# Second expert stage of a two-layer transformer kernel: second products four pairs behind, work grouped in PSUM banks

## The reference, cut to what matters

```python
logits = -dist2 + jnp.einsum('bld,ed->ble', x, rw) + rb
topv, topi = jax.lax.top_k(logits, TOP_K)            # TOP_K = 4 of E = 16
w = jax.nn.softmax(topv, axis=-1)
hidden = jax.nn.gelu(jnp.einsum('bld,efd->blef', x, w1) + b1, approximate=False)
exp_out = jnp.einsum('blef,edf->bled', hidden, w2) + b2
fused = jnp.sum(w[..., None] * take_along_axis(exp_out, topi[..., None], axis=2), axis=2)
```

## Time and profile before

| | us |
|---|---|
| three runs, median | 649.49 |
| lowest and highest of the three | 643.33, 649.77 |
| profiled execution, its own time (the span) | 724.3 |
| of it, from 461 us to 701 us: second expert stage | 240 |

### The profile page before, as it was taken

The page is one execution under the profiler, slowest core; times in us unless marked ns, Lnnn a source line. Parts: engine busy times, 40 slices in busy tenths (PEclk is TensorE's granted clock), DMA queues, the critical chain, the costliest instruction groups (busy, mean ns, idle before and its releaser), DMA issues.

```text
span 724.3 us, 15939 instructions
## 1 busy us (share of the span) xinstructions
PE 551.5 (76%) x4812; PEld 383.9 (53%) x4812; DVE 446.3 (62%) x1659; ACT 363.8 (50%) x972; POOL 323.3 (45%) x429
## 2 busy tenths in 40 slices
PE   5789999994129736899999992598877787759980
PEld 2234445443018734445554451387766686759880
DVE  5678889835752237678999658576544554423257
ACT  2158888841005634388998732144433343335543
POOL 3755765130025755624333424444555544554440
PEclk9999999975558975689999965589999889978995
DMA  6520620021001261750400010434433333334473
GB/s 179 150 65 11 185 58 1 2 44 19 1 12 43 39 142 63 213 167 10 124 2 2 2 44 18 138 123 131 133 120 116 110 122 115 126 101 155 163 234 112
DMA packets 65734, 65.11 MB, mean 90 GB/s; under 512 B 16259, under 2 KB 46099, under 8 KB 65526
## 3 DMA queue, kind: packets, MB, share of 16 engines
q1 hardware_dynamic: 58390, 52.49, 22.9%
q0 software_dynamic: 7264, 11.62, 6.6%
HBM read 29.77 MB, written 11.87 MB: 57 GB/s over the span
## 4 chain that ended last, share of the span: by engine, by line
PE 56%; DVE 14%; issue 7%; another core or an unknown queue 7%; ACT 7%; POOL 3%; SPq 3%; DMA 2%; DVEq 0%; ACTq 0%; POOLq 0%
PE bank L896 9%; PE bank L1311 8%; PE bank L1301 7%; PE bank L879 6%; PE bank L861 4%; ACT queries L1600 3%; PE bank L913 3%; DVE passed L1882 2%; ACT prob L1423 2%; PE bank L1097 2%; PE bank L937 1%; PE bank L1255 1%; PE bank L1109 1%; POOL sum L761 1%
## 5 line engine op out<-in xcount | busy, mean ns | idle before, releaser
L1700 DVE TENSOR_REDUCE mx<-bank 128x2 f32<-128x512 f32 x256 | 163.3, 685 | 37.7 <-PE bank L861 35.9
L1423 ACT ACTIVATE prob<-bank 128x512 f32<-128x512 f32 x256 | 142.1, 601 | 42.0 <-PE bank L879 37.3
L1600 ACT ACTIVATE queries<-bank,prob 128x128 f32<-128x128 f32 x316 | 90.1, 377 | 137.2 <-remote 65.5
L1301 PE MATMUL bank<-keys,prob 128*128 x632 | 98.1, 305 | 14.1 <-ACT keys L1592 12.0
L1301 PEld LDWEIGHTS bank<-keys,prob 128*128 128x128 f32 x632 | 88.2, 216 | 19.3 <-issue 18.4
L774 POOL DMA_INDIRECT prob<-xs,idx_g x64 | 61.7, 964 | 80.4 <-DVE idx_g L2113 23.5
L1311 PE MATMUL bank<-W,queries 128*128 x632 | 94.6, 296 | 3.4 <-issue 1.9
L1311 PEld LDWEIGHTS bank<-W,queries 128*128 128x128 f32 x632 | 83.6, 205 | 5.6 <-issue 3.3
L783 POOL DMA_INDIRECT parts<-augs,idx_s x64 | 63.2, 987 | 45.8 <-DVE augs L2154 23.3
L896 PE MATMUL bank<-prob,augs 128*32 128x256 f32 x1024 | 82.5, 409 | 1.4 <-ACT prob L1423 1.4
L861 PE MATMUL bank<-keys,queries 32*128 32x256 f16 x512 | 78.2, 294 | 4.2 <-DVE mx L1700 2.0
(11 more groups left out here) (272 smaller groups left out, 1017.3 us busy)
## 6 DMA issues: line engine op xcount, KB each, us to landing
prob<-W SPq DMA_DIRECT2D x79, 258.0 KB
W<-in_w SPq DMA_DIRECT2D x48, 256.0 KB, 3.7
sum<-zero SPq DMA_DIRECT2D x3, 1024.0 KB, 9.5
xr<-XT SPq DMA_DIRECT2D x12, 128.0 KB, 2.0
xs<-X SPq DMA_DIRECT2D x2, 768.0 KB, 5.7
prob<-xs,idx_g POOLq DMA_INDIRECT x80
XB<-sum SPq DMA_DIRECT2D x1, 1024.0 KB, 5.1
Y<-sum SPq DMA_DIRECT2D x4, 256.0 KB, 5.8
```

What stands on the lines that cost most here:

```text
L1301: last = nc.tensor.matmul(bank[2 + p % 2][:, P * f:P * f + P], wc[:, p % 4, P * f:P * f + P], xsT2[:, bass.ds(at, 1), :], start=True, stop ...
L1423: nc.scalar.activation(prob[:, v % 8, :, :], st_bank(b, v)[:, :], ACT.Exp, scale=SCALE).then_inc(exp_done, 1)
L1600: last = nc.scalar.activation(hid2[:, p % 4, f, :], bank[2 + p % 2][:, P * f:P * f + P], ACT.Gelu, bias=wc[:, p % 4, WB + f:WB + f + 1])
L1700: nc.vector.tensor_reduce(m_at, bank[S1B[u % 2]][:, :].rearrange("p (j k) -> p j k", j=2), AX.X, ALU.max).then_inc(s1_used, 1)
```

## The change

- The second product of pair p moves from step p + 2 to step p + 4 (SKEW). First products get four PSUM banks (2 to 5) instead of two, so first product p waits for gelu p - 4. The hidden activations get eight buffers instead of four (`queries` and `XT`), since gelu p now waits for second product p - 8.
- Turns are grouped: tiles 0 and 1 alone, then [2, 3], [4, 5], [6, 7], then fours. A group is transposed into one bank and copied by one ACT instruction. The group [8..11] is turned at step 6, and the next ones at 9, 11, 14, 17 and 20; from tile 32 on a group that starts with tile t is turned at step t - 3.
- Lists from tile 6 on go in groups of three in one bank: three lists every two steps to tile 32, then three every three steps. One copy and one conversion serve three.
- Outputs are grouped: four second products go to one bank, and DVE adds the four pairs at the step that is five after the group's last pair, once the last of the four is there. The last groups are [76, 77] and [78].
- Buffers move to make room (`gateT`, `hit`, the third slice of choices). SP's load of that slice waits for first product 62. The order on POOL and SP is as before, their waits too but for that one.

```diff
-def turn_step(t):
-    if t < RING:
-        return -1 if t == 0 else -((12 - 11 * t) // 16)
-    return min(t - 2, 21 - -(4 + 11 * (t - 31)) // 8)
-def list_step(t):
-    if t < 6:
-        return -1
-    return 2 * (t - 6) // 3 if t < RING else t - 14
+TURN_GROUPS = [[0], [1], [2, 3], [4, 5], [6, 7]] + [list(range(t, t + 4)) for t in range(8, NJT[1], 4)]
+FIRST_LISTS, PER_LIST = 6, 3
+LIST_GROUPS = [list(range(t, min(t + PER_LIST, NJT[1]))) for t in range(FIRST_LISTS, NJT[1], PER_LIST)]
+OUT_GROUPS = [list(range(p, p + 4)) for p in range(0, 76, 4)] + [[76, 77], [78]]
+SKEW, HRING, HIDRING = 4, 4, 8
+def turn_step(group):
+    t = group[0]
+    if t < 8:
+        return {0: -1, 1: 0, 2: 1, 4: 3, 6: 4}[t]
+    return -((1 - 11 * t) // 16) if t < RING else t - 3
+def list_step(g):
+    return 2 * g if g < 9 else 3 * g - 8
+SUMS = {p: [g for g, group in enumerate(OUT_GROUPS) if group[-1] + SKEW + 1 == p] for p in range(NPAIR + SKEW + 1)}
...
+            def row_turns(group):
+                wait_for(pe, rows_in, group[0])
+                for i, t in enumerate(group):
+                    row_fetched(pe, t)
+                    nc.tensor.transpose(bank[0][:, P * i:P * i + P], xg[:, t % XRING, 0:P],
+                                        ident[:, :]).then_inc(row_turned, 1)
...
             def pair_first(e, p):
-                if p >= 2:
-                    pe.wait_ge(pair_gelu, p - 1)
+                if p >= HRING:
+                    pe.wait_ge(pair_gelu, p - HRING + 1)
...
             def pair_second(e, p):
                 pe.wait_ge(pair_gelu, p + 1)
-                if p >= 2:
-                    pe.wait_ge(pair_added, p - 1)
+                g, i = OUT_OF[p]
+                if i == 0 and g >= 2:
+                    pe.wait_ge(pair_added, OUT_GROUPS[g - 2][-1] + 1)
...
-                for p in range(NPAIR + 2):
+                for p in range(NPAIR + SKEW):
...
-                    if p >= 2:
-                        pair_second(expert.pop(p - 2), p - 2)
+                    if p >= SKEW:
+                        pair_second(expert.pop(p - SKEW), p - SKEW)
...
-            def pair_sum(s, p):
+            def pair_sum(s, p, g):
-                dve.wait_ge(pair_out, p + 1)
+                dve.wait_ge(pair_out, OUT_GROUPS[g][-1] + 1)
...
-                    if p >= 2:
-                        e = pair_expert(dve, words, p - 2)
-                        s = pair_slot(dve, e, p - 2)
-                        pair_gated(e, s, p - 2)
-                        pair_sum(s, p - 2)
+                    for g in SUMS[p]:
+                        for n in OUT_GROUPS[g]:
+                            e = pair_expert(dve, words, n)
+                            s = pair_slot(dve, e, n)
+                            pair_gated(e, s, n)
+                            pair_sum(s, n, g)
```

More of the change, by code:

```diff
@@ L194, in program @@
         yo = rt[:, 4 * P:8 * P].rearrange("p (b c) -> p b c", c=P)
[L195 removed]
+        hid2 = [h[:, :].rearrange("p (s f c) -> p s f c", s=4, f=NF)[:, s, :, :] for h in (queries, XT) for s in range(4)]
         xsT2 = keys[:, :].rearrange("p (t c) -> p t c", c=P)
@@ L1316, in pair_steps @@
             def pair_steps():
-                for t in LISTS[-1]:
+                for t in range(FIRST_LISTS):
+                    if t >= 2:
+                        pe.wait_ge(row_ready, t - 1)
                     row_list_of(t)
@@ L1322, in pair_steps @@
                 words = pair_tables(pe, pe_words)
-                for t in TURNS[-1]:
-                    row_turn(t)
+                for group in TURNS[-1]:
+                    row_turns(group)
                 expert = {}
-                for p in range(NPAIR + 2):
+                for p in range(NPAIR + SKEW):
                     if p < NPAIR:
@@ L1606, in pair_steps @@
                 for p in range(NPAIR):
-                    for t in TURNS[p - 1]:
-                        row_in(t)
+                    for group in TURNS[p - 1]:
+                        rows_copied(group)
                     pair_hidden(p)
@@ new lines, in rows_listed @@
+            def rows_listed(g):
+                t0, n = LIST_GROUPS[g][0], len(LIST_GROUPS[g])
+                dve.wait_ge(row_list, t0 + n)
+                if g == 0:
+                    dve.wait_ge(row_ready, t0)
+                for t in LIST_GROUPS[g]:
+                    row_hits(t)
+                ends_of = bank[1][:, 0:(P + 2) * n].rearrange("p (t c) -> p t c", c=P + 2)[:, :, P + 1]
+                nc.vector.tensor_copy(slot_expert[:, t0:t0 + n], ends_of).then_inc(lstep, 1)
+                dve.wait_ge(lstep, NJT[0] + 2 * FIRST_LISTS + (PER_LIST + 1) * g + n + 1)
+                at = t0 % (2 * PER_LIST)
+                nc.vector.tensor_copy(idx_g[:, t0:t0 + n], tok[:, at:at + n, 0]).then_inc(row_ready, n)
```

112 lines of the change are left out of this document (65 added, 47 removed).

## The result

| | us |
|---|---|
| before, four runs beside those of the change: median, range | 646.41 (642.87 to 649.77) |
| the change, four runs: median, range | 669.87 (666.28 to 672.46) |
| ratio, with its 95% interval | 1.0344 (1.0277 to 1.041) |
| profiled execution of the change, its span | 667.3 |

The change is slower by 22 us by the ratio and 23.5 by the medians. A ratio leaves out runs more than 1.5% above the fastest of their kernel and a median doesn't, so the two can differ by 2 to 3 us. The forecast was 662, 12.3 us slower, in a range from 645 to 668: the direction was right, the size was about half.

The account below looks back on a forecast made before the run. PE and POOL were taken as level near full use, POOL's 1.29 us per indirect DMA deciding. Later sums and turn waits put the last scatter at 642.8 against 630.5, so 649.5 + 12.3 = 662 us, range 645 to 668.

Parts of the forecast that it names:

- The runs have none of the late releases: Second expert stage: waits where PE was done but others learned late (46 us of PE idle) are nearly absent from runs.
- The supposition on what lies ahead of this stage: First expert stage, ahead of the second: supposed disturbed by the same waits; no size given.
- The profiled span falls because four banks absorb the late releases: Four banks and the longer skew absorb these waits, so profiled span falls from 724.3 to some 690 to 715.
- Start and steps to 24: Second expert stage: step 3 starts 2 us earlier; step 18 at 504.6 against 506.6, step 24 at 516.3.
- Early turns starve PE, 2.8 us: Early turns in groups of four: waiting for gathers stalls PE 0 to 5 us in all, taken as 2.8.
- Sums in fours: "Nothing", but later: DVE lags 3 us at most, costing nothing; but sum 15 comes at step 20, sum 16 at step 24.
- Why scatter 1 is late: POOL: scatters 1 to 4 wait for sums 16 to 19; scatter 1 at 517.5, where before scatter 0 started at 507.9.
- POOL's 1.29 us per DMA up to gather 63: POOL issues DMAs back to back, 1.29 us each: 61 from scatter 1 put gather 63 at 596.2.
- Turns from tile 32 on: PE waits for gathers at turned groups: 1.6 us at [36..39], then 2.2 at each of the six that follow.
- The first rival: POOL keeps up: a DMA takes under 1.04 us, no turn waits, no change; 647 us (643 to 655), chance 0.24.
- the second (faster): Waits of the two-bank scheme are in the runs too, the change removes them: 640 us (625 to 643), chance 0.12.
- The third: Early turns starve PE as well, 5 us in place of 2.8, plus half clock: +16 to +20, 667 us, chance 0.12.

Follow-up runs that it names:

- the repeated profile: The kernel before, unchanged, profiled again: 647.66 us beside 648.13, ratio 0.9989, span 647.0.
- c3: The change itself, run again in a later session where every kernel was slower: 735.42 us beside 723.77 for before, ratio 1.0222.
- a1: The change with sums one by one, at the step of their second product: 660.02 us beside 646.59 for before, ratio 1.0236.
- a3: The change with sums one by one and turns from tile 32 on at step t - 1: 658.88 us, ratio 1.0251 to before.
- a4: The change with single sums, turns from tile 32 on at step t - 1 and a skew of two pairs: 657.22 us, ratio 1.0181 to before.
- a8: The change with three 128x128 fills on POOL ahead of each scatter: 719.88 us beside 649.1 for before, ratio 1.1123.
- b3: The kernel before with one 128x128 fill on POOL ahead of each scatter: 652.58 us beside 648.13, ratio 1.0101.
- a6: The change, single sums, skew two, groups from tile 32 turned at before's step for their last tile or earlier t - 1: 652.89 us, ratio 1.0079.
- a2: The change with turns from tile 32 on at step t - 1 in place of t - 3: 668.7 us, without a ratio.
- a7: The change with single sums, skew two, earlier turns of groups from tile 32 on, and 11 gathered tiles in flight: 652.47 us, ratio 1.0061 to before.
- a9: The change with single sums, skew two, turns in twos at before's step for the second tile: 722.9 us beside 719.56, ratio 1.0038.
- d1: The change with single sums, skew two, turns in twos and 11 gathered tiles: 720.75 us beside 714.33 for before, ratio 1.0097.

## Why the prediction was right in sign and half in size

**The runs have none of the late releases.** Right, and now seen: the repeated profile has no such wait. What was not seen is that an execution of this kind can be that of a whole session, runs and profile alike. Whether the first profile was taken in the session of its runs is not on record. The supposition on what lies ahead of this stage was right: 9.3 us of the 77.3 lie there.

**The profiled span falls because four banks absorb the late releases.** Wrong, though the span fell. The two executions were of different conditions. Like beside like, the span goes from 724.3 to 732.1 (c3) and from 647.0 to 667.3, and ACT's remote waits from 65.5 us to 85.9 (44.4 + 41.5). The stage loses 14.8 us there (240.3 to 255.1) and 17.9 in the quick condition.

**Start and steps to 24.** Right as differences. Step 3 was to start 2 us earlier: 10.8 against 12.6. Step 18 was put 2.0 us ahead of before: 1.7. The levels were too low, by 2.6 and 2.9 us at step 18 (45.7 against 48.3, 43.7 against 46.6), since I took 2.2 us a step from 3 to 18, and before takes (48.3 - 12.6)/15 = 2.38.

**Early turns starve PE, 2.8 us.** Mis-sized, harmless: 0.8.

**Sums in fours: "Nothing", but later.** This is the step that failed: beyond the later scatter 1 it put the sums in fours at nothing, and its sum for the end (four second products, 3.6, and 1.4 for sum and issue) has no wait for a burst in it. Single sums alone give 7 to 9.9 us of run and 6.5 of the stage, 3.8 of them behind gather 63 (a1). Three parts of the stage were missing. DVE was said to lag by 3 us at most. Sum 15 was due at step 20 (first product at 501.30 here), and ends at 507.53 + 0.35, 6.6 us later, of which the burst itself is some 3; so scatter 0 leaves at +58.0 and scatter 1 at +60.9 where +56.6 was said, 3.2 us of it from the steps before. Behind gather 63, bursts held POOL four times, 12.1 us in all, the last time for 4.74 us with 15 scatters still to go at 1.28 or more. And a bank of four held second product 78 for 2.15 us. From second product 78 to the last scatter I had 2.3 us (0.9 + 1.4), it took 6.1. Before has a slow end too: POOL has a queue of scatters there, the last four come 1.6 to 1.8 apart, and scatter 0 to 63 take 125.4 us where 122.6 was said.

**Why scatter 1 is late.** The price was nearly right, the reason in part. The forecast had scatter 1 at 56.6 in place of 49.6 (scatter 0 at 47.0, and 2.58), 7.0 us later. Measured are 60.9 against 52.7, 8.2. But single sums give back only 2.4 of it (a1); with single sums, a skew of two gives back 5.8 (a3 to a4).

**POOL's 1.29 us per DMA up to gather 63.** Right to the tenth: 78.7 us for 61 intervals. a8 shows that the rest follows it one to one (31.1 us more on POOL, first product 78 33.5 later). Before has little slack there: in b3, 2.8 us more on POOL put gather 63 back by 2.1 and first product 78 by 1.0. The Trainium skill (DMA: Bandwidth & Descriptors, section on the anatomy of one DMA by the SWDGE path) says that descriptor generation is small and that many descriptors can be emitted before it shows. For indirect DMAs of 128 rows these runs disagree: each takes 0.97 to 1.00 us of POOL's time.

**Turns from tile 32 on.** Forecast 1.6 us and six times 2.2, 14.8 in seven groups; measured 11.3 in eight, gather 39 still last to land at its group. Landing took 3.53 us from the gather's start in place of 2.71.

The sum, on the scale after first product 0: forecast 181.9 for the last scatter, measured 193.5, 11.6 over: 3.2 at step 24, 1.1 more at scatter 1, 0.9 in landing, 0.4 to first product 78, 2.2 and 3.8 at the end. Before was built 6.0 too low as well (169.6 against 175.6), which hid half of the error: the difference is 17.9 in place of 12.3. Of these 5.6 us, 1.4 have come up by gather 63 (8.4 us later than in before, forecast 7.0), and 4.2 arise behind it, where the bursts are. The spans differ by 2.4 more, outside this stretch: from the last scatter on 23.1 us against 19.8, and first product 0 came 0.9 us earlier. In the other traces of the quick condition that end took 19.7 to 23.3 us, for kernels of either kind, so I leave these us to the execution.

**The turns, which no step of the prediction priced alone.** With sums single and skew two, 9 us remain (a4). Without the 7.6 us hold of gather 40, gather 63 comes 6.8 us earlier (139.0 to 132.2), the last scatter 5.4 and the run 4.3 (a4 to a6, different chips; ratios 1.0181 and 1.0079). In the change itself the hold doesn't show: POOL there comes to gather 40 late enough. In a3, which turns tile 32 two steps later, POOL waits 2.46 us ahead of gather 40, which starts 0.3 us after the masks of tiles 32 to 35. That is why a2 and a1 together gave little more than a1:

```profile
525.64 0.97 POOL L796 DMA_INDIRECT prob<-xs,idx_g  x1 [2.46 <-issue]
```

After a6, 4 to 5 us of run stay open. The waits for copies of turned groups, 8.1 us in the stage against 3.7 in before, are the candidate, with lists in threes and the four banks as the others. No run in the quick condition tests it.

The first rival (POOL keeps up, no change) and the second (faster) are out. The third landed nearest the time, 667, but by none of its reasons: early turns cost 0.8 us. No version tried beats before by more than its interval: the nearest, before with a ring of 11, is at 0.9964 (0.992 to 1.0007).

## What to carry to other kernels

Lists in threes saved DVE 10 us of work here, on an engine that waits anyway; sums in fours saved it none, and delayed every member of a batch, the first most. Price a batch by when its last member is ready, by who is queued for the first, and once more at the end of the stage, where nothing follows to hide it. A group that shares a ring with its producer must leave it as early as its members did one by one, or the producer stands for the whole group (7.63 us in a4). Where the profiled span and the runs differ by 11%, profile the kernel before once more ahead of any build-up: both levels of the forecast, and the wait that seemed to be gained, hung on it.

## What the runs showed of the hardware

- The kernel before takes 647 us in some sessions and 714 to 724 in others, in one case on the same chip number (0: 646.59, later 719.56), and all runs of a session are of its kind but for three outliers: 1154.84 us (a7), 1154.77 (a9) and 1520.95 (d1). In the slow ones ACT and DVE wait again and again, up to 12.0 us at a time (c3), for work of PE whose recorded end lies well before. PE itself does not run on as usual: in c3, from 564 to 569 us, while that gelu waits, it starts the matmuls of a second product one by one, with up to 1.19 us idle between them, which the profile calls issue. What switches the condition, no run tells.
- One fill on POOL before each scatter costs 0.09 us, three in a row cost 1.01, at 0.21 to 0.22 us of busy time each. A scatter has 0.30 us of idle time before it anyway. With one fill 0.17 us are left of it (b3); with three, the fills take 0.80 us and 0.52 to 0.57 us of idle time still follow (a8).
